# Fifty unread products at the head of TensorE's queue in the first stage of a two-layer attention and expert kernel

## The chip, the core and the metric

The kernel runs on one core of a Trainium2 chip. The metric is the device time of one execution in microseconds (us). Engines are named as in the profile: PE (TensorE) does the matrix products, DVE (VectorE) the elementwise work and reductions, ACT (ScalarE) the copies and functions, POOL (GpSimd) more elementwise work, SP (SyncE) issues the transfers.

## The reference

x has 8 batches of 256 rows of 128 numbers, ctx the same shape. Four blocks are added to x one after the other:

```python
x = x + L0_xattn(_layernorm(x), ctx, ctx, mask, w_q, w_k, w_v, w_o)    # 16 heads of 8
x = x + L0_ffn(_layernorm(x), ...)       # 32 experts, the best 6 of each row, and a shared one
x = x + L1_xattn(ctx, _layernorm(x), ...)                               # 16 heads of 64
x = x + L1_ffn(x, router_w, W1, b1, W2, b2)                             # 8 experts, one of them per row
```

What matters here is the beginning of the first: `Q = layernorm(x) @ w_q.T`, `K = ctx @ w_k.T`, `V = ctx @ w_v.T`, and the mask, from which each row's bias is made.

## The kernel before

The program is five stages, each a block of instruction streams, one stream per engine, with a barrier of all engines between blocks. The stages are project_layer0, attend_layer0, experts_layer0, attend_layer1 and experts_layer1. The change is in project_layer0, whose streams are L147 to L295.

**Operands.** A product in f32 accuracy is made of three f16 products: every operand is split into a high part (an f16 copy) and a low part (the difference). The helper `three` (L214) issues them: high x high, low x high, high x low, into one bank of PSUM (512 f32 columns).

**Jobs.** The list `jobs` (L135 to L138) sets PE's order: k0, k1, k2, k3, t0, t1, q0, t2, q1, t3, q2, q3, v0 to v3. A k or q job is three products of 512 columns. A t job is four transposes of 128 columns that turn a normed group of x. A v job is four times three products of 128 columns. Job n writes bank n mod 8; from n = 8 on PE waits until the bank has been read.

**Who follows whom.** After each job ACT copies the bank to f16 (L210; for v to f32, L207), and signals hi_done. DVE then forms the low part from the bank and the high part, `low(n)` (L267), and signals lo_done. v has no low part. A q job waits for the copy and the low of its t job. SP stores the parts of k and q to DRAM (L160) and loads them back in another layout (L303), for the next stage.

**DVE's order** (L269 to L295) is: statistics of x (L69, L72), var, a reciprocal after ACT's square root (root_done), norm(0), the split of the weights and of ctx (w3_hi, ctx_lo, w3_lo, L277 to L281; these are the "operands"), norm(1), low(0) to low(4), norm(2), low(5), low(6), norm(3), low(7) to low(11), and bias_k (L295). norm(g) makes the bias of a group of four row tiles from its mask (L257) and then the normed rows (L82); t jobs wait for it.

**PE's first waits.** The first job waits for operands to reach 3, that is for w3_lo. The identity matrices come from POOL early (L86 to L94, and L194, which makes the third signal of ident_done).

**The next stage** begins, behind the barrier, with PE's row_scores_of (L411) and DVE's 16 maxima (L586), then a transfer of the maxima by SP (L364), then the attention proper.

Of the kernel before, what the change touches and what calls it, by code (L numbers as in the profile page):

```python
# [20 lines left out]
P = 128  # L21
# [75 lines left out]
def project_layer0(nc, io, keep):  # L97
# [3 lines left out]
    with ExitStack() as ctx:  # L101
# [3 lines left out]
        def sem(name):  # L105
            return ctx.enter_context(nc.semaphore("a_" + name))

        xr, nrm, ident32, ident16 = keep["xr"], keep["nrm"], keep["ident32"], keep["ident16"]
# [10 lines left out]
        banks = [ctx.enter_context(nc.psum_tensor(f"a_bank{i}", [P, 512], F32)) for i in range(8)]  # L119
# [4 lines left out]
        made, ident_done = sem("made"), sem("ident_done")  # L124
        var_done, root_done = sem("var_done"), sem("root_done")
# [15 lines left out]
        def lows(n):  # L141

            return sum(1 for kind, _ in jobs[:n + 1] if kind != "v")
# [68 lines left out]
        @block.tensor  # L212
        def _(pe):
            def three(out, a_hi, a_lo, b_hi, b_lo):  # L214
                pe.matmul(out, a_hi, b_hi, start=True, stop=False)
                pe.matmul(out, a_lo, b_hi, start=False, stop=False)
                return pe.matmul(out, a_hi, b_lo, start=False, stop=True)

            for n, (kind, g) in enumerate(jobs):
                bank = banks[n % 8]  # L220
                if n >= 8:

                    pe.wait_ge(hi_done, n - 7)
                    pe.wait_ge(lo_done, lows(n - 8))
                cols = slice(512 * g, 512 * g + 512)
                if kind == "k":
                    pe.wait_ge(operands, 3)
                    mm = three(bank[:], w3_hi[:, 1, :], w3_lo[:, 1, :], ctx_hi[:, cols], ctx_lo[:, cols])
                elif kind == "q":
                    pe.wait_ge(hi_done, order[("t", g)] + 1)  # L230
                    pe.wait_ge(lo_done, lows(order[("t", g)]))
                    mm = three(bank[:], w3_hi[:, 0, :], w3_lo[:, 0, :], x_hi[:, cols], x_lo[:, cols])
                elif kind == "v":
                    for i in range(4):
                        t = slice(512 * g + P * i, 512 * g + P * i + P)
                        mm = three(bank[:, P * i:P * i + P], ctx_hi[:, t], ctx_lo[:, t], w3_hi[:, 2, :], w3_lo[:, 2, :])
                else:
                    pe.wait_ge(ident_done, 2)
                    pe.wait_ge(norm_done, g + 1)
                    for i in range(4):  # L240
                        mm = pe.transpose(bank[:, P * i:P * i + P], nrm[:, 4 * g + i, :], ident32[:])
                mm.then_inc(bank_ready, 1)
# [2434 lines left out]
```

## Time and profile before

| | us |
|---|---|
| median of 3 runs | 1161.09 |
| lowest and highest of them | 1159.34 and 1166.76 |
| the profiled execution | 1165.66 |
| its span, first to last instruction | 1163.8 |

The mean granted clock of TensorE over the span is 0.935 of full speed. The profile is of one execution. In it PE is busy 962.2 us, DVE 855.8, ACT 793.1 and POOL 641.2. The first stage, which the change is in, is the first 41.5 us of the 1163.8. A time line counts from the span's start. Busy shares are averages over all stages; what the change is worth has to be read from the waits and the timeline of its stage.

### The profile page before, as it was taken

What the parts mean: (1) busy time and instruction counts of PE and PEld (TensorE: products, weight loads), DVE (VectorE), ACT (ScalarE), POOL (GpSimd) and SP (SyncE); (2) the same over time, 40 slices, a digit from 0 to 9 for tenths busy, and PEclk for the clock granted to TensorE, in tenths of its full rate; (3) what the DMA queues carried; (4) which work ended last, traced back from release to release, by engine and by line L of the source; (5) the groups of instructions that cost most, each with busy time, mean ns of one, the idle gap of its engine ahead of it and who ended that gap; (6) DMA issues with size and microseconds to landing.
All of it is one profiled execution on the core that took longest, in us unless ns stands there. A gap on an engine that the chain in (4) does not pass through costs nothing. (4 is left out here: it accounts for less than half of the span.)

```text
span 1163.8 us, 26435 instructions
## 1 busy us (share of the span) xinstructions
PE 962.2 (83%) x9571; PEld 617.0 (53%) x9571; DVE 855.8 (74%) x2003; ACT 793.1 (68%) x1567; POOL 641.2 (55%) x572
## 2 busy tenths in 40 slices
PE   2699899557999965699988988998898888769885
PEld 1366666423444432266666666666666667644374
DVE  7778787457666677588888898888889887567731
ACT  2277887777545453599899898989989897743031
POOL 4145444432778843376678675667866566302425
PEclk9899999866999986799999999999999999969898
DMA  7411110040000001011111011111101111060150
GB/s 266 74 15 17 24 20 0 4 153 8 21 21 26 14 1 24 10 25 29 29 29 29 15 24 21 29 29 29 30 15 25 19 30 29 2 249 1 48 145 23
DMA packets 76241, 46.55 MB, mean 40 GB/s; under 512 B 55160, under 2 KB 73063, under 8 KB 75310
## 3 DMA queue, kind: packets, MB, share of 16 engines
q1 hardware_dynamic: 74696, 42.32, 15.3%
q0 software_dynamic: 1440, 2.82, 0.7%
q8 instruction: 67, 1.10, 0.4%
q14 instruction: 38, 0.31, 0.1%
HBM read 26.44 MB, written 8.77 MB: 30 GB/s over the span
## 5 line engine op out<-in xcount | busy, mean ns | idle before, releaser
L1551 POOL TENSOR_TENSOR e_p_lo<-e_probs,e_p_hi 128x1024 f16<-128x1024 f32 x64 | 136.4, 2132 | 119.8 <-ACT e_probs L1844 119.8
L1910 DVE TENSOR_REDUCE e_neg_max<-e_row_scores 128x1 f32<-128x512 f32 x256 | 167.2, 681 | 7.2 <-PE e_row_scores L1623 6.0
L1842 ACT ACTIVATE e_p_hi<-e_scores 128x512 f16<-128x512 f32 x256 | 152.6, 596 | 10.2 <-PE e_scores L1727 7.2
L1534 POOL TENSOR_TENSOR e_raw<-e_raw,e_inv 128x512 f32<-128x512 f32 x90 | 93.3, 1044 | 74.1 <-DVE e_inv L1882 74.1
L404 POOL TENSOR_TENSOR b_p_lo<-b_probs,b_p_hi 128x512 f16<-128x512 f32 x64 | 74.0, 1156 | 96.8 <-ACT b_probs L555 95.8
L1639 PE MATMUL e_mix<-e_v_cols,e_p_hi 128*128 128x65 f16 x1024 | 108.1, 193 | 21.1 <-POOL e_p_lo L1551 20.5
L1726 PE MATMUL e_scores<-e_q_stack,e_k_stack 128*128 128x256 f16 x512 | 124.1, 274 | 0.2 <-DMA e_q_high<-e_neg_rows 0.2
L1727 PE MATMUL e_scores<-e_q_high,e_k_high 128*128 128x256 f16 x512 | 123.7, 273 | 0.0
L1639 PEld LDWEIGHTS e_mix<-e_v_cols,e_p_hi 128*128 128x128 f16 x1024 | 95.1, 96 | 34.6 <-POOL e_p_lo L1551 31.4
L1623 PE MATMUL e_row_scores<-e_k_high,e_q_high 65*128 65x512 f16 x256 | 97.8, 389 | 17.3 <-DVE e_neg_max L1910 14.8
L797 POOL TENSOR_TENSOR c_h_lo<-c_hidden,c_h_hi 128x512 f16<-128x512 f32 x68 | 78.7, 1157 | 55.8 <-ACT c_h_hi L1003 54.7
L1640 PE MATMUL e_mix<-e_v_cols,e_p_hi 128*128 128x64 f16 x1024 | 108.0, 195 | 0.0
L1641 PE MATMUL e_mix<-e_v_cols,e_p_lo 128*128 128x65 f16 x1024 | 107.5, 192 | 0.0
L1546 POOL TENSOR_TENSOR e_natural<-e_raw,e_natural 128x512 f16<-128x512 f32 x90 | 102.4, 1158 | 6.2 <-ACT e_natural L1773 6.2
L1915 DVE TENSOR_TENSOR e_p_lo<-e_scores,e_p_hi 128x512 f16<-128x512 f32 x128 | 87.4, 683 | 19.8 <-ACT e_scores L1847 19.8
L1640 PEld LDWEIGHTS e_mix<-e_v_cols,e_p_hi 128*128 128x128 f16 x1024 | 95.3, 97 | 5.5
L1641 PEld LDWEIGHTS e_mix<-e_v_cols,e_p_lo 128*128 128x128 f16 x1024 | 95.5, 99 | 0.0
L586 DVE TENSOR_REDUCE b_neg_max<-b_row_scores 128x2 f32<-128x512 f32 x128 | 82.5, 685 | 15.5 <-PE b_row_scores L421 13.2
L552 ACT ACTIVATE b_p_hi<-b_scores 128x1024 f16<-128x1024 f32 x64 | 65.8, 1028 | 34.7 <-PE b_scores L441 32.8
L1773 ACT CAST e_natural<-e_raw 128x512 f16<-128x512 f32 x96 | 59.1, 616 | 39.8 <-POOL e_raw L1538 20.6
L1050 ACT ACTIVATE c_gated<-c_gate_ps 128x512 f32<-128x512 f32 x64 | 38.2, 597 | 65.9 <-PE c_gate_ps L845 65.9
L1608 PE MATMUL e_misc<-ident,e_natural 128*128 128x128 f16 x768 | 61.3, 225 | 25.3 <-POOL e_natural L1546 12.9
(399 smaller groups left out, 2905.4 us busy)
## 6 DMA issues: line engine op xcount, KB each, us to landing
e_k_high<-e_k_stack SPq DMA_DIRECT2D x64, 128.0 KB, 2.6
e_q_high<-e_q_stack SPq DMA_DIRECT2D x32, 128.0 KB, 2.6
w<-in_w SPq DMA_DIRECT2D x2, 2048.0 KB, 10.3
c_w<-in_w SPq DMA_DIRECT2D x17, 192.0 KB, 2.4
placed_scratch<-in_no_rows SPq DMA_DIRECT2D x1, 2313.0 KB, 18.8
a_mask_q<-in_mask_q SPq DMA_DIRECT2D x4, 512.0 KB, 7.9
a_mask_k<-in_mask_k SPq DMA_DIRECT2D x1, 2048.0 KB, 14.4
parts_scratch<-a_parts SPq DMA_DIRECT2D x8, 256.0 KB, 2.4
```

The source lines that it names most:

```text
L1534: nc.gpsimd.tensor_tensor(raw[par][:, j], raw[par][:, j], bc(inv[:, HU * j:HU * j + HU], (P, HU, D1), 2), ALU.mult).then_inc(normed, 1)
L1546: nc.gpsimd.tensor_tensor(natural[:, j, :, at], raw[par][:, j], natural[:, j, :, hi], ALU.subtract).then_inc(low_done, 1)
L1551: nc.gpsimd.tensor_tensor(p_lo[buf][i][:], probs[i][:], p_hi[buf][i][:], ALU.subtract).then_inc(lo_done[i], 1)
L1623: pe.matmul(row_scores[qt % RBANKS][:], q_high[par][0:MASK1 + 1, h, P * qt:P * qt + P], k_high[par][0:MASK1 + 1, h, :], start=True, stop=T ...
L1639: pe.matmul(out, p_hi[buf][i][:, kt, at], values[:, 0:D1 + 1], start=first, stop=False, skip_group_check=True)
L1640: pe.matmul(out[:, 0:D1], p_hi[buf][i][:, kt, at], values[:, D1 + 1:2 * D1 + 1], start=False, stop=False, skip_group_check=True)
L1641: mm = pe.matmul(out, p_lo[buf][i][:, kt, at], values[:, 0:D1 + 1], start=False, stop=last, skip_group_check=True)
L1726: pe.matmul(out, k_stack[hf][:, h, cols], q_stack[hf][:, h, :], start=(kt % 2 == 0), stop=False, skip_group_check=True)
L1727: mm = pe.matmul(out, k_high[hf][:, h, cols], q_high[hf][:, h, :], start=False, stop=True, skip_group_check=True)
L1842: act.activation(p_hi[p % 2][i][:, at, :], scores[n % SBANKS][:], ACT.Exp).then_inc(exp_done, 1)
L1910: dve.tensor_reduce(neg_max[buf][:, 2 * i + qt:2 * i + qt + 1], row_scores[qt % RBANKS][:], AX.X, ALU.max, negate=True).then_inc(max_done, 1)
L1915: dve.tensor_tensor(p_lo[buf][i][:, at, :], scores[n % SBANKS][:], p_hi[buf][i][:, at, :], ALU.subtract).then_inc(lo_done[i], 1)
```

## The change

Ahead of the loop over the jobs, PE now waits for all three signals of the identities and for ACT's square root. Then it does 50 products of ident16 by ident16, 128 columns each, into the first 128 columns of bank 7. Nothing reads them; bank 7 is later overwritten by job 7 (t2). Each product is written as one call, which loads its weights anew. The other engines' streams are as before.

```diff
@@ -216,6 +216,11 @@
                 pe.matmul(out, a_lo, b_hi, start=False, stop=False)
                 return pe.matmul(out, a_hi, b_lo, start=False, stop=True)
 
+
+            pe.wait_ge(ident_done, 3)
+            pe.wait_ge(root_done, 1)
+            for _ in range(50):
+                pe.matmul(banks[7][:, 0:P], ident16[:], ident16[:], start=True, stop=True)
             for n, (kind, g) in enumerate(jobs):
                 bank = banks[n % 8]
                 if n >= 8:
```

## Rows read from the trace of the kernel before

**Rows 1.** The page: busy time and share; granted clock in 40 slices, tenths.

```profile
PE 962.2 (83%) x9571; PEld 617.0 (53%) x9571; DVE 855.8 (74%) x2003; ACT 793.1 (68%) x1567; POOL 641.2 (55%) x572
...
PEclk9899999866999986799999999999999999969898
```

**Rows 2.** Waits, 19 to 42 us: who <- whom: us in total, times, longest.

```profile
PE a_bank L215 <- DVE a_w_lo L281: 19.5, 1, 19.5
...
ACT a_parts L210 <- PE a_bank L217: 11.1, 8, 5.8
...
DVE a_parts L267 <- ACT a_parts L210: 2.9, 5, 1.0
```

**Rows 3.** Timeline to 20.4: start, us, engine, line, operation [idle before <-releaser].

```profile
2.10 0.55 POOL L194 TENSOR_SCALAR ident_m<-ident 128x128 f16<-128x128 f32 x1
...
13.20 0.21 ACT L201 ACTIVATE a_var<-a_var 128x16 f32<-128x16 f32 x1 [11.17 <-DVE a_var L272]
...
18.92 0.55 DVE L281 TENSOR_TENSOR a_w_lo<-a_w,a_w_hi 128x384 f16<-128x384 f32 x1
...
19.52 0.61 PE L215 MATMUL a_bank<-a_ctx_hi,a_w_hi 128*128 128x512 f16 x1 [19.52 <-DVE a_w_lo L281]
...
20.35 0.63 PE L217 MATMUL a_bank<-a_ctx_lo,a_w_hi 128*128 128x512 f16 x1
```

**Rows 4.** Timeline, 21 to 28 us.

```profile
21.02 0.59 ACT L210 CAST a_parts<-a_bank 128x512 f16<-128x512 f32 x1 [5.82 <-PE a_bank L217]
...
22.09 0.68 DVE L267 TENSOR_TENSOR a_parts<-a_bank,a_parts 128x512 f16<-128x512 f32 x1
...
24.62 1.25 PE L241 MATMUL a_bank<-ident,nrm 128*128 128x128 f32 x8
...
24.86 0.59 ACT L210 CAST a_parts<-a_bank 128x512 f16<-128x512 f32 x1 [0.69 <-PE a_bank L217]
...
25.48 0.69 DVE L267 TENSOR_TENSOR a_parts<-a_bank,a_parts 128x512 f16<-128x512 f32 x1 [0.59 <-ACT a_parts L210]
26.09 0.69 DVE L267 TENSOR_TENSOR a_x_lo<-a_bank,a_x_hi 128x512 f16<-128x512 f32 x1
...
26.92 0.38 PE L215 MATMUL a_bank<-a_x_hi,a_w_hi 128*128 128x512 f16 x1 [1.06 <-DVE a_x_lo L267]
...
27.14 0.38 PE L216 MATMUL a_bank<-a_x_hi,a_w_lo 128*128 128x512 f16 x1
...
27.77 0.59 ACT L210 CAST a_parts<-a_bank 128x512 f16<-128x512 f32 x1 [1.23 <-PE a_bank L217]
```

**Rows 5.** Windows: stretch, length, busy (x) by engine, granted clock, DMA share, GB/s.

```profile
20.00:30.00 10.00, 7.05 (x27) 3.32 (x25) 8.53 (x31) 4.00 (x7) 0.00 (x0) 1.00 0.46 129
...
34.00:35.00 1.00, 1.00 (x5) 0.63 (x4) 0.57 (x1) 0.36 (x1) 0.00 (x0) 0.50 0.00 0
```

**Rows 6.** Timeline, 37 to 42 us: the v groups and the stage's end.

```profile
37.33 0.31 PE L215 MATMUL a_bank<-a_w_hi,a_ctx_hi 128*128 128x128 f16 x1
...
38.51 0.31 PE L217 MATMUL a_bank<-a_w_lo,a_ctx_hi 128*128 128x128 f16 x1
...
38.71 0.22 PE L216 MATMUL a_bank<-a_w_hi,a_ctx_lo 128*128 128x128 f16 x1
...
38.85 2.60 ACT L207 COPY v_all<-a_bank 128x512 f32<-128x512 f32 x4 [0.69 <-PE a_bank L217]
...
41.90 0.38 PE L419 MATMUL b_row_scores<-k_stack,q_stack 128*128 128x256 f16 x2 [1.08 <-PEq L101]
```

**Rows 7.** Timeline of PE: the transposes of t3.

```profile
33.52 1.08 PE L241 MATMUL a_bank<-ident,nrm 128*128 128x128 f32 x4 [2.49 <-DVE nrm L82]
```

**Rows 8.** Timeline, 42 to 63 us: the beginning of the second stage.

```profile
42.54 11.04 DVE L586 TENSOR_REDUCE b_neg_max<-b_row_scores 128x2 f32<-128x512 f32 x16 [1.45 <-PE b_row_scores L421]
...
56.65 0.61 PE L419 MATMUL b_row_scores<-k_stack,q_stack 128*128 128x256 f16 x2 [2.73 <-DMA q_stack<-b_neg_rows]
...
62.60 0.38 PE L439 MATMUL b_scores<-q_stack,k_stack 128*128 128x256 f16 x2
```

## Prediction

> **What bounds the kernel now.** I read the page first: PE is busy 83% of the span, and its granted clock falls below 9 tenths in only some of the 40 slices [rows 1]. That is an average over five stages, and the edit touches only the first, which ends at 41.9 us. So I read next the waits of 19 to 42 us, then the timeline of that stretch.
>
> In the waits [rows 2], look for who waits in a chain. PE sits idle for the first 19.5 us until DVE has formed w3_lo. After that ACT waits for PE (11.1 us in 8 waits) and DVE waits for ACT (2.9 us in 5). DVE never waits for ACT longer than 1.0 us at once: from 19.4 us on, DVE is nearly the bound, and PE only where its slow products hold up the copies that DVE needs.
>
> In the timeline the chain is this. The square root on ACT ends at 13.41; DVE forms the first operands until 19.47; PE's first product starts at 19.52 [rows 3]. The first and the third start at 19.52 and 20.35, so 0.42 us apart; 512 columns in 0.42 us is the 1.2 GHz level. The products of q0 start at 26.92 and 27.14, 0.22 us apart, the 2.4 GHz level [rows 4]. The granted clock reads 1.00 for 20 to 30 us [rows 5], although the products of 19.5 to 24.6 us run at the low level; where the same products run 0.42 us apart later it reads 0.50 (34 to 35 us). So in the first 25 us I trust the spacing of the products and not the clock row.
>
> DVE is free for low(0) at 22.09, after norm(1); it then takes the five lows, low(0) to low(4), the last two at 25.48 and 26.09. low(1) to low(3) are paced by ACT's copies of k1 to k3, and these by slow products: ACT's four copies start from 21.02 to 24.86, 1.28 us apart, three products of 0.42 us [rows 4]. From 26.09 to about 34.5 DVE runs without a gap.
>
> **The change, part by part.** Nothing is removed or moved. Two waits and 50 products of 128 columns are added at the head of PE's queue. Nothing else is queued on PE before its first real product, and nothing waits for these 50: they signal no semaphore, and bank 7, which they write, is first used by the transposes of t2 at 29.62.
>
> *The waits.* ident_done reaches 3 when POOL ends its L194 at 2.65; root_done comes at 13.41 [rows 3]. So the products start at about 13.5.
>
> *The products.* The nearest rows are the first twelve products of the v groups, also 128 columns of f16 with a weight load each: they start from 37.33 to 38.51, (38.51 - 37.33) / 11 = 0.107 us apart, with the loads hidden [rows 6]. 50 x 0.107 = 5.4 us, which ends at 18.9. That is 0.6 us before the first operand is ready at 19.5. Cost on the path: nothing. The cover is PE's idle time of 19.5 us; without it they would cost up to 5.4 us. Bounds of one product: 0.055 us (a quarter of the 0.22 us that 512 columns take at the high level [rows 4]) and 0.31 us, the whole duration of one, if they did not overlap. The first ends sooner; the second is a rival below. I take 0.107, since nothing but the operands differs.
>
> *What it may bring: the clock.* In this trace PE three times worked on at the low level and came to the high one. Work began at 19.52 and the level was high by the transposes of 24.62, eight of which took 1.25 us (5.1 us later) [rows 3, 4]. It began again at 33.52 and the level rose between 38.51 and 38.71, where durations fall from 0.31 to 0.22 us (5.1 us later) [rows 6, 7]. It began at 56.65 with 0.61 us for two products of 256 columns and was up when the same pair took 0.38 us at 62.60 (at most 6.0 us later) [rows 8]. With work from 13.5 on, the rise should come at 18.6 to 19.5, before the first real product.
>
> *What the high level is worth.* With k0 to k3 at 0.216 us a product instead of 0.427, a group takes 0.65 instead of 1.28 us. k0 is then complete about 0.85 us after 19.52 (as q0: start 26.92, its copy at 27.77 [rows 4]), at 20.4. ACT's copies of 0.59 us start at about 20.4, 21.0, 21.7, 22.3, and that of t0 at 22.9. Each lies before the time at which DVE wants it. low(0) cannot start before 22.09: it stands behind norm(1), which does not wait for PE. Then low(0) to low(4) run back to back at 0.60 us apart (the spacing of 25.48 and 26.09, where DVE waits for nobody): 22.09, 22.69, 23.29, 23.89, 24.50. low(4) started at 26.09; the gain is 26.09 - 24.50 = 1.6 us. PE itself saves more, 12 x 0.211 = 2.5 us by the start of t0; the 0.9 us between turn into waiting, since DVE has norm(1) and five lows of its own work in the way.
>
> *What is late next.* norm(2), low(5), low(6), norm(3), low(7) and low(8) follow on DVE without a wait, so all move by 1.6 us, and so do the transposes of t3 (33.52), which wait for norm(3) [rows 7]. SP's stores wait for the lows and move with them; the load of q_stack, issued from 35.08 behind the store of q1, moves to 33.5. It is ahead of the stage's end either way. The stage ends at 41.45 with the last of four copies of v on ACT, which start at 38.85 and run 2.60 us back to back; stage two's first product starts at 41.90 [rows 6]. Between t3 and these copies PE's slow products are again on the path, and here the shift may not come through in full. If the level rises 5.1 us after the work resumes, v moves by 1.6 us. If it rises at about 38.6 as before, more of v lies below it: the copies of v then start at 37.3, 38.6, 39.3 and 40.0 and end at 40.6, a gain of 41.45 - 40.6 = 0.85 us. I take 1.6 us, since two of three lags are 5.1 us; 0.85 stays as the near bound. If the level had not fallen at all before t3 (it was 0.50 at 34 us [rows 5]), t3, q3 and v0 would be faster by 0.45, 0.63 and 0.63 us, 1.7 us more: the far bound is 3.3 us.
>
> In stage two DVE's 16 maxima (11.04 us from 42.54 [rows 8]) are the bound and move as a block. Then PE waits 2.7 us for a transfer, and resumes at the low level, at 56.65, until about 62.5 [rows 8]. A shift does not remove this; the lag of 5.1 to 6.0 us may come out otherwise, worth (6.0 - 5.1) / 2 = 0.45 us each way. There are more such spells later (the slices that read 6 and 7 [rows 1]); the shift adds or takes a few tenths at each.
>
> **Sum.** 1163.8 us of span and 1.9 us around it made 1165.7 us in the profiled execution. Against it: -1.6 us, so 1164.1. The median of the runs, 1161.09, stands 4.6 us below that execution, and the gain does not depend on what differs between them: 1161.1 - 1.6 = 1159.5 us. What a measurement of this kernel can tell from no change is about 1%, 11.6 us; the runs of before themselves lie from 1159.34 to 1166.76.
>
> **The rivals.**
> - *The gain is given back before the barrier of 41.5 us.* For: the v groups are paced by the level. Against: two equal lags of 5.1 us. Time: 1161.1 - 0.85 = 1160.2 us at the near bound, 1161.1 if it is all given back.
> - *The 50 products do not lift the level, or too late.* To fail in full, the rise would have to come as late as now, at 24.6. The gain is whole if it comes by about 20.9 (k1 must be copied by 22.7), which is 7.4 us after 13.5; no row shows more than 6.0. The Trainium skill, "TensorE: Matmul & The Clock Gate", section "The HAM clock gate", says that one kernel can show a different number of slow products from run to run, so the rise need not keep its distance from the first product. By that rule some executions would gain less than 1.6 us and some the same; no two executions stand in this trace to show it. Time of this rival: 1161.1 us.
> - *Slower: the products do not overlap.* All 50 write the same columns of one bank, each as a fresh start. At 0.31 us each they last 15.5 us, to 29.0, and the first real product starts 9.5 us late. low(0) then starts at 29.0 + 0.85 + 0.59 = 30.4 instead of 22.09, 8.3 us late, less the 1.6 us of the high level: +6.7 us, 1167.8 us. It decides from a spacing of 0.174 us: the products then end at 22.2 and low(0) starts at 23.7, 1.6 us late, which eats the gain. Against: groups of three into one bank overlap at 0.107 and 0.42 us spacing [rows 3, 6].
> - *More than the sum.* The shift lets the level stay up before t3 or rise one spell sooner at 56.65: 3.3 us, 1157.8 us.
>
> **How the numbers follow.** The forecast (1.6 us, 1159.5) has 0.50; given back 0.18; no lift 0.15; more than the sum 0.12; not overlapping 0.05. All of these lie within 1% of 1161.1 us. For the sides beyond 1% there are only spells of the low level later in the kernel, many of which would have to come out alike: 0.02 faster, 0.02 slower, 0.96 within. The range takes the cases from 1157.8 to 1161.1 and about 3 us of the spread that the runs of before show on both sides, since a median of few runs carries it: 1155.0 to 1164.5 us; 1167.8 is left out with its 0.05.
>
> **What would show it.** Right: 50 products from 13.5, the first about 0.107 us apart, over by 19; k0 to k3 0.216 us apart from 19.5; low(0) to low(4) back to back from 22.1; DVE without a wait on ACT there; t3 at about 31.9; the last copy of v ending at 39.9 to 40.6; stage two's first product at 40.3 to 41.1 instead of 41.90. Wrong: k products still 0.42 us apart; the first of them after 19.6; low(0) later than 22.1; or stage two starting at 41.9 all the same. What would overthrow the forecast as a whole is a difference of more than 2 us that arises behind 65 us.

## The result and the profile after

The changed kernel takes 1167.96 us (median of 20 runs, 1160.66 to 1172.26), the kernel before 1159.61 us (median of 20). The ratio is 1.0063, with a 95% interval of 1.0053 to 1.0074: by it about 7.3 us slower (the two medians differ by 8.4). It was forecast 1.6 us faster, 1159.5 us, with a range up to 1164.5. The profiled execution of after took 1169.58 us, with a span of 1167.8.

The page of after: busy time, and the granted clock in 40 slices.

```profile
PE 973.2 (83%) x9621; PEld 625.3 (54%) x9621; DVE 856.4 (73%) x2003; ACT 793.5 (68%) x1567; POOL 640.9 (55%) x572
...
PEclk9799989957999985699999999999999999959889
```

PE has the 50 products more and is busy 11 us longer; DVE and ACT do the same work as before. A slice is 29.2 us long, and stage two fills the second to the eighth. Two of them are lower than in [rows 1]: the second reads 7 instead of 8 and the sixth 8 instead of 9; the eighth is higher, 9 instead of 8. That is a first hint of where to look.

The timeline of after, in the first stage: start, us, engine, line, operation [idle before <-releaser].

```profile
13.55 5.49 PE L223 MATMUL a_bank<-ident 128*128 128x128 f16 x50 [13.55 <-ACT a_var L201]
...
19.51 0.39 PE L215 MATMUL a_bank<-a_ctx_hi,a_w_hi 128*128 128x512 f16 x1 [0.47 <-DVE a_w_lo L286]
...
19.74 0.38 PE L216 MATMUL a_bank<-a_ctx_hi,a_w_lo 128*128 128x512 f16 x1
...
20.37 2.53 ACT L210 CAST a_parts<-a_bank 128x512 f16<-128x512 f32 x4 [5.18 <-PE a_bank L217]
...
22.08 2.48 DVE L272 TENSOR_TENSOR a_parts<-a_bank,a_parts 128x512 f16<-128x512 f32 x4
...
24.47 0.68 DVE L272 TENSOR_TENSOR a_x_lo<-a_bank,a_x_hi 128x512 f16<-128x512 f32 x1
...
31.89 1.08 PE L246 MATMUL a_bank<-ident,nrm 128*128 128x128 f32 x4 [1.53 <-DVE nrm L82]
...
36.76 2.60 ACT L207 COPY v_all<-a_bank 128x512 f32<-128x512 f32 x4 [0.23 <-PE a_bank L217]
...
39.91 0.38 PE L424 MATMUL b_row_scores<-k_stack,q_stack 128*128 128x256 f16 x2 [1.17 <-PEq L101]
```

Up to the transposes of t3 the first stage does what was forecast. The products are over at 19.04, the first real one starts at 19.51, and its successors are 0.22 us apart where [rows 3] show 0.42. DVE takes low(0) to low(3) in one piece from 22.08 and low(4) at 24.47, against 26.09 in [rows 4]. The transposes of t3 start at 31.89 instead of 33.52 [rows 7]. Stage two's first product comes 2.0 us earlier than in [rows 6], a little more than the 0.8 to 1.6 us that were named.

The loss comes later. SP's queue tells it best: the maxima are sent once in each of stage two's steps, in two transfers of 4 KB one behind the other (the x2 in the lines). Its issues in the kernel before, from SP's timeline:

```profile
97.82 1.14 SPq L364 DMA_DIRECT2D q_stack<-b_neg_rows  x2
...
119.00 1.15 SPq L364 DMA_DIRECT2D q_stack<-b_neg_rows  x2
...
140.09 1.14 SPq L364 DMA_DIRECT2D q_stack<-b_neg_rows  x2
...
161.29 1.15 SPq L364 DMA_DIRECT2D q_stack<-b_neg_rows  x2
```

The same in after:

```profile
96.97 1.14 SPq L369 DMA_DIRECT2D q_stack<-b_neg_rows  x2
...
121.37 1.15 SPq L369 DMA_DIRECT2D q_stack<-b_neg_rows  x2
...
142.46 1.14 SPq L369 DMA_DIRECT2D q_stack<-b_neg_rows  x2
...
167.73 1.14 SPq L369 DMA_DIRECT2D q_stack<-b_neg_rows  x2
```

From one such pair to the next, before needs 21.2, 21.1 and 21.2 us; after needs 24.4, 21.1 and 25.3. Two steps have become 3.2 and 4.1 us longer. In between lies the start of a step, where PE waits for both transfers. PE's timeline at these starts, in the kernel before:

```profile
100.29 0.39 PE L419 MATMUL b_row_scores<-k_stack,q_stack 128*128 128x256 f16 x2 [0.66 <-DMA q_stack<-b_neg_rows]
...
142.57 0.39 PE L419 MATMUL b_row_scores<-k_stack,q_stack 128*128 128x256 f16 x2 [0.67 <-DMA q_stack<-b_neg_rows]
```

And in after:

```profile
101.06 0.60 PE L424 MATMUL b_row_scores<-k_stack,q_stack 128*128 128x256 f16 x2 [2.27 <-DMA q_stack<-b_neg_rows]
...
123.75 0.39 PE L424 MATMUL b_row_scores<-k_stack,q_stack 128*128 128x256 f16 x2 [0.57 <-DMA q_stack<-b_neg_rows]
...
146.85 0.61 PE L424 MATMUL b_row_scores<-k_stack,q_stack 128*128 128x256 f16 x2 [2.58 <-DMA q_stack<-b_neg_rows]
```

Read the bracket: PE is idle 2.27 and 2.58 us at two of the starts, where before has 0.66 and 0.67. And read the duration: after these waits the two products of the line take 0.60 instead of 0.39 us, the low level. The windows of after from 101 to 104 us say the same, a granted clock of 0.50, where before has 1.00:

```profile
101.00:104.00 3.00, 2.94 (x11) 1.64 (x12) 1.71 (x3) 0.00 (x0) 0.46 (x1) 0.50 0.68 76
```

So each long wait costs twice: 1.6 to 1.9 us by itself and another 1.6 to 2.2 us by the low level behind it. Stage three starts at 229.80 in before and 236.25 in after, 6.5 us late. From there to the end, after takes 931.6 us and before 934.0; the 14 traces lie between 925.7 and 934.0 there, so no loss shows behind stage two.

### The profile page after: what moved, and what is told of

It reads as the page before. It is cut to its first block and busy times, and to the rows that moved or that the text cites. A ratio compares the mean times of both kernels' runs of the same rounds, so it can differ in the third digit from the quotient of the medians.

```text
span 1167.8 us, 26536 instructions
## 1 busy us (share of the span) xinstructions
PE 973.2 (83%) x9621; PEld 625.3 (54%) x9621; DVE 856.4 (73%) x2003; ACT 793.5 (68%) x1567; POOL 640.9 (55%) x572
## 5 line engine op out<-in xcount | busy, mean ns | idle before, releaser
L1613 PE MATMUL e_misc<-ident,e_natural 128*128 128x128 f16 x768 | 61.3, 225 | 24.2 <-POOL e_natural L1551 12.2
```

## The experiments

All kernels are told together here, since they answer each other; "added" is the number of instructions added to PE's stream, counting a product as two (its weight load and itself). "First" is the start of stage two's first product in the record. The three steps run from one issue of the maxima to the next, in the one profiled execution of each kernel; 21.2, 21.1 and 21.2 us is the undisturbed length. "Ratio" is the time over that of before, with its 95% interval.

| kernel | added | ratio | first, us | three steps, us |
|---|---|---|---|---|
| before | 0 | 1 | 41.90 | 21.2, 21.1, 21.2 |
| before_again | 0 | single run, 1160.42 us | 40.26 | 21.2, 21.1, 21.2 |
| after | 100 | 1.0063 (1.0053 to 1.0074) | 39.91 | 24.4, 21.1, 25.3 |
| after_again | 100 | single run, 1166.16 us | 40.90 | 24.5, 21.1, 25.2 |
| e_obs | 100 | single run, 1163.93 us | 39.67 | 24.2, 21.1, 24.5 |
| e_hold | 100 | 1.0065 (1.0044 to 1.0087) | 41.61 | 24.5, 21.1, 22.8 |
| e_early | 100 | 1.0082 (1.0057 to 1.0107) | 40.55 | 25.6, 21.1, 21.2 |
| e_tiny | 100 | 1.0073 (1.0055 to 1.0091) | 40.34 | 21.2, 21.1, 24.8 |
| e_tail | 100 | 1.0075 (1.0049 to 1.0101) | 40.65 | 21.2, 21.1, 24.7 |
| e_tiny25 | 50 | 1.0023 (0.9995 to 1.0052) | 42.24 | 24.2, 21.1, 22.8 |
| e_bhold | 0 | 1.0010 (0.9995 to 1.0025) | 42.82 | 21.2, 21.1, 22.8 |
| e_wide | 26 | 0.9996 (0.9982 to 1.0009) | 40.39 | 22.8, 21.1, 21.2 |
| e_pad | 254 | 0.9994 (0.9982 to 1.0007) | 39.93 | 21.2, 21.1, 21.2 |
| e_tiny127 | 254 | 0.9999 (0.9980 to 1.0018) | 41.29 | 21.2, 21.1, 21.2 |

The steps and the ratio do not speak of the same executions. The profiled executions of e_tail, e_tiny and e_hold took 1160.39, 1161.44 and 1162.33 us, each the fastest run of its kernel, whose medians are 1169.79, 1168.12 and 1166.18 us. Their steps show which disturbance occurs, not that it makes up the whole of the median's loss.

### Is it the earlier start of stage two?

before_again is the kernel of before, unchanged.

> The kernel of before once more, for a second record of its clock. In its first profile the granted clock was at the high level without a break from 62.6 to 223 us; in the changed kernel's profile it fell at 77.0, 100.9 and 145.3 us. Theory A (the falls belong to the changed kernel's timing): this record again has no fall between 63 and 220 us. Theory B (the falls come and go from execution to execution, and the two profiles differ by chance): this record has one or more there. Time 1158 to 1163 us by both.

Its record has one spell of the low level at 77.0 us and none from there to 220 us, and no long wait. It took 1160.42 us. It showed one thing that matters below: stage two starts at 40.26, not 41.90.

e_hold delays stage two of the changed kernel:

```diff
+        spare = sb("spare", [P, 3, 512], F16)
...
                 act.copy(out[:, 512 * g:512 * g + 512], banks[n % 8][:]).then_inc(hi_done, 1)
+            for i in range(3):
+                act.copy(spare[:, i, :], banks[7][:])
```

> The changed kernel, with ACT doing three more copies of 0.65 us (into a tile that nothing reads) behind the last copy of v, so that stage two starts at about 41.9 us as before, 2.0 us later than in the changed kernel. Theory A1 (the earlier start of stage two brings the falls of the clock): the falls are gone, and the time is that of before, 1160 us, against 1168. Theory A2 (the 50 products at the head of PE's stream bring them, wherever stage two starts): the time stays near 1168 or rises by the 2.0 us to 1170. Theory A3 (any shift can bring or take falls): some other value between 1157 and 1172, with falls at other places.

e_bhold has the same edit on the kernel of before.

> The kernel of before with the same three extra copies on ACT and no added products: stage two starts at about 43.9 us, 2.0 us later than before. Theory A2 (the products are the cause): 1160 + 2 = 1162 us, and no falls of the clock between 65 and 220 us. Theory A3 (any shift can bring or take falls): the difference to before is clearly not 2.0 us, and the record shows falls in stage two.

e_early lets the 50 products run before ACT's square root:

```diff
             pe.wait_ge(ident_done, 3)
-            pe.wait_ge(root_done, 1)
```

> The changed kernel without the wait for the square root: the 50 products run from about 2.7 to 8.1 us, so PE idles for 11 us before its first real product, and the low level is back by then. k0 to k3 then run 0.42 us apart, stage one ends at about 41.5 us and stage two starts at 41.9 as before. Theory A1 (earlier start of stage two): 1160 us. Theory A2 (the products at the head, their code or their place in the stream): 1168 us, with falls in stage two.

e_hold starts stage two at 41.61 and is as slow as after, with a wait of 2.59 us at 102.29. e_early has k0 to k3 at the low level again, and its median is 8 us above before. The three copies delayed stage two by 1.5 us and not by the 2.0 expected (in e_bhold ACT ends with v at 40.91 and with the copies at 42.38). e_bhold is 1.2 us slower than before, with an interval from 0.6 us faster to 2.9 slower, which fits that delay and one of none. So neither the start of stage two nor the level in stage one is the cause. What the slow kernels share is the 50 products in PE's stream. The theory of the shift fell.

One reading of the step column is already possible. e_bhold has a spell of the low level at 143.6 us without a long wait, and that step takes 22.8 us: the spell alone costs 1.6 us.

### Is it PE's early work or its code?

after_again is the changed kernel once more.

> The changed kernel once more, for a second record. In its first one PE waited 2.3 us at the start of the third step of stage two (b = 2, first product at 101.06) and 2.6 us at that of the fifth (146.85), where the kernel of before waits 0.6 us, and the clock fell at both. Theory C (the wait is for PE's own code: about 100 added instructions move where the pieces of code end) expects the wait at the third step again. Theory B (chance) expects no wait over 0.8 us there. Time 1165 to 1171 us by C.

It has the waits at the same two steps, 2.53 us at 100.27 and 2.51 at 145.82.

e_tiny keeps the instructions and takes away the work:

```diff
-                pe.matmul(banks[7][:, 0:P], ident16[:], ident16[:], start=True, stop=True)
+                pe.matmul(banks[7][0:16, 0:16], ident16[:, 0:16], ident16[:, 0:16], start=True, stop=True)
```

> The changed kernel with its 50 products cut to 16 rows of weights by 16 columns: the same number of instructions at the head of PE's stream, but hardly any work, so that the clock should not rise before k0. k0 to k3 run 0.42 us apart, stage two starts at 41.9 us as before. Theory C (the added code is what costs): the long waits at the steps of stage two are there, and the time is 1167 to 1170 us, the 1168 of the changed kernel and up to 2 us for the lost gain. Theory D (PE's early work, through the clock's history, is what costs): 1160 to 1161 us, as before.

e_pad keeps the 50 products and adds 77 tiny ones ahead of the wait for the square root:

```diff
             pe.wait_ge(ident_done, 3)
+            for _ in range(77):
+                pe.matmul(banks[7][0:16, 0:16], ident16[:, 0:16], ident16[:, 0:16], start=True, stop=True)
             pe.wait_ge(root_done, 1)
```

> The changed kernel with 77 more products of 16 by 16 ahead of the wait for the square root. With them some 254 instructions are added and not 100. The trace shows PE's code coming in pieces of 16 KB; at 64 bytes an instruction, an assumption, that is 256 of them, so the pieces end nearly where they did before. Theory C: the long waits at the steps of stage two are gone, stage one still gains 2 us, and the time is 1157 to 1159 us. Theory D (PE's early work): 1168 us as with 50 products. If only the count of added instructions mattered, 1168 or more.

e_wide does the same work in fewer instructions:

```diff
-            for _ in range(50):
-                pe.matmul(banks[7][:, 0:P], ident16[:], ident16[:], start=True, stop=True)
+            for _ in range(13):
+                pe.matmul(banks[7][:], ident16[:], ident16[:].unsqueeze(1).to_broadcast((P, 4, P)), start=True, stop=True)
```

> 13 products of 512 columns instead of 50 of 128: the same time at the low level (13 x 0.427 = 5.5 us), and 26 instructions instead of 100. The clock should rise as in the changed kernel and stage two start at 39.9 to 40.3 us. Theory C: the code moves by a quarter as much; if that misses the step's start, 1157 to 1160 us, if not, 1168. Theory D (PE's early work): 1168 us.

The answer is clear. 50 products of 1.40 us in all (e_tiny) cost as much as 50 of 5.49 us. The 50 full products with 77 more (e_pad) cost nothing that the runs can tell. So it is not PE's early work but the length of the code that decides, and not in proportion: with 26 and 254 added instructions the time is that of before within 0.2%, with 100 it is 7 to 9.5 us more. e_pad came out at 1159.98 us, above the 1157 to 1159 expected of it.

The next three test this without any full product. e_tiny127 and e_tiny25 are e_tiny with 127 and 25 products. e_tail puts 50 tiny ones at the end of stage one's stream and none at its head:

```diff
                 mm.then_inc(bank_ready, 1)
+            pe.wait_ge(hi_done, 9)
+            pe.wait_ge(lo_done, lows(8))
+            for _ in range(50):
+                pe.matmul(banks[0][0:16, 0:16], ident16[:, 0:16], ident16[:, 0:16], start=True, stop=True)
```

> As the kernel with 50 products of 16 by 16, but 127 of them: some 254 added instructions where that has 100, and again hardly any work. The two differ in the length of the code alone. Theory C (where the pieces of PE's code end decides): 1160 to 1161 us, as before, and no long wait at the steps of stage two. If more added code costs more: above 1168 us.

> 25 products of 16 by 16 at the head: some 50 added instructions. The 13 wide products added 26 and cost nothing, 50 tiny ones added 100 and cost 7 us. Theory C says only that the cost is that of a wait at a step's start or nothing, so near 1161 or near 1165 to 1168 us, and that the record shows a long wait in the second case and none in the first. A cost in proportion to the added instructions would give 1164.5 without a long wait.

> The kernel of before with 50 products of 16 by 16 behind PE's last product of v, at the end of stage one's stream, and none at its head. The code of stage two moves by about 100 instructions as in the changed kernel, that of stage one not at all. Theory C: 1167 to 1169 us, with a long wait at the third or the fifth step of stage two. Theory E (it is what comes at the head of the stream that matters): 1160 to 1161 us, or 0.5 us more if the added products outlast ACT's copies.

e_tiny127 and e_tiny differ in 77 tiny products alone, and the longer one is faster by 8 us. The waits of 60 to 223 us show it, first e_tiny, then e_tiny127 (us in total, times, longest):

```profile
PE b_row_scores L424 <- DMA q_stack<-b_neg_rows: 6.2, 6, 3.0
```

```profile
PE b_row_scores L424 <- DMA q_stack<-b_neg_rows: 3.8, 6, 0.7
```

e_tail is as slow as the kernels with products at the head, so the head has no part in it: what counts is that stage two's code has moved. e_tiny25 lies between; its 12 runs spread from 1155.92 to 1172.31 us, so its executions differ among themselves, as do those of e_tail (1160.39 to 1175.4), and its interval reaches from nothing to 0.5%. Its record has the long wait once.

### What does the code collide with?

The page lists two DMA queues for instructions, before and after alike. One of them, q8, has 67 packets and 1.10 MB, so 16 KB each. That they are PE's code is read from the experiments: with 254 instructions more in PE's stream alone (e_pad, e_tiny127) there are 68, and the places of q8's packets move with PE's code.

```profile
q8 instruction: 67, 1.10, 0.4%
```

Narrowing the DMA view to short windows shows when a piece of 16 KB starts. In after one starts at 98.55 and one at 144.50. The DMA view of after from 96.5 to 101 us (queue: packets, MB, share; issue: count, KB, median us to landing):

```profile
q8 instruction: 1, 0.02, 1.5%
...
q_stack<-b_neg_rows SPq DMA_DIRECT2D x2, 4.0 KB, 2.5
```

In before, from 97.5 to 101 us, there is no line of q8, and the transfer lands sooner:

```profile
q_stack<-b_neg_rows SPq DMA_DIRECT2D x2, 4.0 KB, 1.7
```

In before the nearest piece starts at 103.08, 2.8 us after the step has begun. In all eleven long waits (of after, after_again, e_hold, e_early, e_tiny, e_tail, e_tiny25 and e_obs, which is told below), one starts 2.2 to 2.8 us before PE resumes.

Two explanations were left: PE waits for its code, or the piece of code holds up the small transfer of the maxima, for which PE waits. e_obs has SP wait for the same transfer as a second witness:

```diff
                 place_max(b + 1)
+                sp.wait_ge(max_in, 16 * QT * (b + 2))
                 if b + RING < B:
```

> The changed kernel, with SP also waiting for the transfer of the maxima (the wait that PE has at a step's start) before it issues the next load of k_stack. SP so is a second witness of when that transfer lands. In the kernels with the cost, a 16 KB piece of PE's code is fetched at about that moment. Theory C1 (PE waits for its code): SP goes on at the usual time, some 2.2 us after the first transfer of maxima is issued, and PE 4.1 to 4.4 us after it. Theory C2 (the piece of code holds up the small transfer, and PE waits for that): SP too goes on late, 0.1 to 0.3 us ahead of PE. Time 1165 to 1171 us by both.

SP's timeline in e_obs, a disturbed step and an undisturbed one:

```profile
95.39 1.14 SPq L369 DMA_DIRECT2D q_stack<-b_neg_rows  x2
99.31 1.00 SPq L308 DMA_DIRECT2D k_stack<-parts_scratch  x3
...
119.55 1.15 SPq L369 DMA_DIRECT2D q_stack<-b_neg_rows  x2
121.82 1.02 SPq L308 DMA_DIRECT2D k_stack<-parts_scratch  x3
```

And PE's:

```profile
99.51 0.39 PE L425 MATMUL b_row_scores<-k_stack,q_stack 128*128 128x256 f16 x2 [2.32 <-DMA q_stack<-b_neg_rows]
...
121.92 0.39 PE L425 MATMUL b_row_scores<-k_stack,q_stack 128*128 128x256 f16 x2 [0.56 <-DMA q_stack<-b_neg_rows]
```

SP goes on 3.92 us after it has issued the maxima in the disturbed step and 2.27 us in the other, and each time 0.1 to 0.2 us ahead of PE. SP does not run PE's code. So the transfer itself lands late, and PE's wait is a true wait for data. The run took 1163.93 us, below the 1165 to 1171 expected.

The single packets of the kept traces show where the time goes. Each transfer of 4 KB is 16 packets of 256 B, each followed by one of 4 B. In before the 32 packets of the second transfer all start within 2.0 us of the first issue. The DMA view of before from 99.57 to 100.12 us, behind the first transfer and ahead of the next loads:

```profile
DMA packets 32, 0.00 MB, mean 8 GB/s; under 512 B 32, under 2 KB 32, under 8 KB 32
```

The same stretch of the disturbed step of after, 98.72 to 99.27 us:

```profile
DMA packets 30, 0.00 MB, mean 7 GB/s; under 512 B 30, under 2 KB 30, under 8 KB 30
```

One packet of 256 B and its follower are missing. They come at about 99.60, when the piece of 16 KB, begun at 98.55, has taken its 1.06 us. It is so in all eleven disturbed steps: 15 of the 16 packets start by 1.95 us after the first issue, and the last one starts within 0.02 us of the end of the piece. In the 101 other steps of stage two in the 14 traces all 16 have started by 2.06 us. So one packet of the transfer stands behind the piece.

## Why the prediction was wrong

**Stage one: right up to t3 in this record.** Start of the products (13.5, measured 13.55), 0.107 us for one at the low level (50 over at 19.04), the level up before k0, low(4) at 24.50 (24.47), t3 at 31.9 (31.89). Behind t3 more came through than was named: the copies ended at 39.36 (39.9 to 40.6), and stage two began 2.0 us earlier (0.8 to 1.6), below the far bound of 3.3. The rival that the products do not overlap was wrong.

**The size of the gain was taken from one execution.** The lags of 5.1 to 6.0 us between PE's start and the rise of the clock all came from one record. In the second record of before, PE starts at 19.51 as well, but the products turn fast at 22.3, 2.8 us later:

```profile
22.05 0.53 PE L215 MATMUL a_bank<-a_ctx_hi,a_w_hi 128*128 128x512 f16 x1
22.42 0.38 PE L216 MATMUL a_bank<-a_ctx_hi,a_w_lo 128*128 128x512 f16 x1
```

Stage two then starts at 40.26. There low(4) starts at 24.93, so the high level from the first product on gains 0.5 us at that point and not 1.6. The records whose k0 starts at the low level (before, before_again, e_early, e_tiny, e_tiny25, e_tiny127) begin stage two at 41.1 us in the mean, with 40.26 and 42.24 at the ends; those with full work on PE ahead of it (after, after_again, e_pad, e_wide) at 40.3, with 39.91 and 40.90. So my estimate of the change's own gain is about 0.8 us, not 1.6; ten records that spread so far do not settle it. A lag of 2.8 us in one record and of 5.1 us in the other agrees with the section on the clock gate which the prediction cited from the Trainium skill, "TensorE: Matmul & The Clock Gate": the number of slow products differs from run to run. e_pad and e_wide, which keep the gain and are rid of the cost, come out 0.7 and 0.5 us below before, with intervals from 2.1 below to 0.8 and 1.0 above: a gain of 0.8 fits, one of none too.

**The step that failed is the cost of the products.** "Cost on the path: nothing" counted their execution alone, and "the bound and move as a block" let stage two pass unchanged. 100 more instructions also move every later piece of PE's code, and in stage two this carried a piece onto the small transfer that releases PE at a step's start. No row of before shows the near miss as a wait, but its DMA view lists the instruction queue and would have shown a piece 2.8 us behind a step's start. The sum by the records of the changed kernel is: -0.8 us (stage one) + 3.3 + 4.0 us (two disturbed steps, after_again; 3.2 + 4.1 in after) = +6.5 us, against 7.3 us measured. In after itself the lead over before was 0.85 us at the issue of 96.97 against 97.82, and with 3.2 and 4.1 us lost it makes the 6.5 us by which stage three starts late. The other slow kernels are not accounted for in this way: e_tail's one disturbed step costs 3.5 us, and its median is 9 us above before, but the record is of its fastest run. That its slower runs have more disturbed steps is likely and not shown.

**The prediction's last sentence held.** It named a difference that arises behind 65 us as what would overthrow it. None of its rivals had that mechanism; the one on the slower side had another.

**What stays open.** The packet that stands behind the piece explains 0.6 to 1.6 us of the delay. The landing is reported 1.1 to 1.3 us after that packet's start, where it takes 0.3 us in undisturbed steps, and this part is not explained. The order that hurts is not known either. Counted from the first issue of the maxima, a piece that started at 1.58 to 2.05 us went with a long wait in ten of eleven steps, one at 2.15 to 2.21 us in none of ten. Later ones should be harmless, since the transfer has landed by 2.25 us in undisturbed steps; three at 2.67 to 2.70 were, but one at 2.61 (e_tiny) was not, and there the last packet was already missing at 1.95. Whether the packet and the piece share an engine of the DMA the traces do not record; that they do is likely. Open too is why the piece at the loop's return (139.7 to 146.6 us, from the end of step b = 3 to b = 4) appears in after, after_again, e_hold, e_early, e_tiny, e_tiny25, e_tail and e_obs, and neither in before, before_again and e_bhold nor in e_pad, e_tiny127 and e_wide.

The Trainium skill has rules that bear on both. "Runtime: NRT & Kernel Launch", section "Instruction fetch mechanics", says that an engine's instructions come in blocks of 16 KiB, which it gives as 256 instructions, over a DMA queue of its own, that crossing a block's end is mostly hidden, and that a taken branch to a block that is no longer held forces a fetch. The size agrees with 1.10 MB in 67 packets, and the 256 with e_pad and e_tiny127, where 254 added instructions leave the pattern as it was. The word on branches would explain the piece at the loop's return; no run here tested it. On "mostly hidden" the runs differ: in after, two of the eight pieces between 58 and 220 us cost 3.2 and 4.1 us.

## What to carry to other kernels

An added instruction has a second price besides its duration: it moves the code behind it. Before calling instructions on an idle engine free, look in the DMA view for the instruction queue's packets and for the small transfers that release the critical engine; if they lie within a few us of each other, try the change with a padded or a shorter form as well (here 13 wide products instead of 50 narrow ones), or a change in an early stage will be judged by an accident in a later one. And a lag of the clock read in one record is one draw: take two records before building a gain of 1 to 2 us on it.

## What the runs showed of the hardware

- A piece of PE's code is one packet of 16 KB and took 0.9 to 1.3 us in the eleven disturbed steps. There one of the 16 packets of a 4 KB transfer starts only when the piece ends, and PE resumes 1.6 to 2.4 us late.
- An idle time of PE of 2.3 to 3.0 us at a step's start was followed by a spell at the low level each time, worth 1.3 to 2.5 us; a spell without the long wait cost 1.6 us (22.8 instead of 21.2 us for the step, in e_bhold, e_wide, e_hold and e_tiny25).
- Shift by about 254 instructions and the time is that of no shift; shift by 100 and it is 0.6 to 0.8% more.
- The rise of the clock came 2.8 us after PE's first product in one execution of before and 5.1 us after it in another.
